# Opening the FFN's up products with the high terms, and moving proj_lo behind chunk 2's statistics

## The reference, cut to what matters

```python
x = L0_attn_x
x = x + 0.5 * ffn(_layernorm(x), W1, b1, W2, b2)        # FFN A
x = x + attn(_layernorm(x), w_qkv, w_out, b_out, proj)  # linear attention in blocks of 32
x = x + 0.5 * ffn(_layernorm(x), W1, b1, W2, b2)        # FFN B

def ffn(h, W1, b1, W2, b2):                             # W1 128x512, W2 512x128
    return relu(h @ W1 + b1) @ W2 + b2

def attn(x, w_qkv, w_out, b_out, proj):                 # 8 heads of 16, proj 8 x 16 x 128
    q, k, v = split(x @ w_qkv.T)                        # by head and block of 32 tokens
    qp, kp = elu(q @ proj) + 1, elu(k @ proj) + 1
    num = qp @ (kp.T @ v)
    return (num / (qp @ kp.sum() + 1e-8)) @ w_out.T + b_out
```

## Time and profile before

| what | us |
|---|---|
| median of 3 runs | 132.45 (132.33 to 132.54) |
| the profiled execution | 132.63 |
| its span on the core | 130.8 |
| PE busy | 120.4 (92% of the span) |
| DVE, ACT, POOL busy | 89.6, 90.0, 49.8 |

### The profile page before, as it was taken

The page is one execution under the profiler, slowest core; times in us unless marked ns, Lnnn a source line. Parts: engine busy times, 40 slices in busy tenths (PEclk is TensorE's granted clock), DMA queues, the critical chain, the costliest instruction groups (busy, mean ns, idle before and its releaser), DMA issues.

```text
span 130.8 us, 4453 instructions
## 1 busy us (share of the span) xinstructions
PE 120.4 (92%) x1895; PEld 97.1 (74%) x1895; DVE 89.6 (68%) x223; ACT 90.0 (69%) x154; POOL 49.8 (38%) x54
## 2 busy tenths in 40 slices
PE   5998999959999997999998999999969999999891
PEld 5887889825759964785985686699647788788891
DVE  6897884395699379769759948952793995437411
ACT  4764285778898686879778887888787774451720
POOL 7637659159139029005304930850000093005300
PEclk9999999999999999999999999999999999999999
DMA  4798400994009300001910000380020000200202
GB/s 108 227 274 223 75 3 0 351 202 93 0 8 351 135 0 0 5 5 41 382 63 0 8 5 0 147 331 9 5 80 5 5 3 5 77 3 0 85 1 80
DMA packets 10123, 11.10 MB, mean 85 GB/s; under 512 B 788, under 2 KB 6296, under 8 KB 10104
## 3 DMA queue, kind: packets, MB, share of 16 engines
q1 hardware_dynamic: 9952, 10.75, 26.5%
q10 hardware_dynamic: 152, 0.07, 0.2%
HBM read 2.03 MB, written 1.05 MB: 24 GB/s over the span
## 4 chain that ended last, share of the span: by engine, by line
PE 67%; DVE 14%; issue 8%; ACT 6%; POOL 3%; POOLq 0%; DVEq 0%
PE G L310 18%; PE wide L336 9%; PE SO L347 6%; ACT expo L643 5%; PE SO L363 5%; PE G L319 4%; PE G L292 3%; DVE feat L829 3%; PE SO L310 3%; PE G L301 3%; PE G L303 2%; PE G L302 2%; POOL rstd L986 2%; PE G L326 2%; DVE stats L795 2%
## 5 line engine op out<-in xcount | busy, mean ns | idle before, releaser
L829 DVE SCALAR_TENSOR_TENSOR feat<-expo,wide 128x1024 f32<-128x1024 f32 x32 | 38.7, 1218 | 18.7 <-ACT expo L643 18.3
L643 ACT ACTIVATE expo<-wide,minus_one 128x1024 f32<-128x1024 f32 x32 | 35.5, 1114 | 9.1 <-PE wide L336 9.0
L986 POOL TENSOR_TENSOR rstd<-var_eps,minus_half 128x4 f32<-128x4 f32 (+1 forms) x15 | 14.4, 962 | 64.8 <-DVE var_eps L802 64.5
L310 PE MATMUL G<-w,hidden 128*128 128x128 f32 x208 | 26.6, 277 | 0.0
L310 PEld LDWEIGHTS G<-w,hidden 128*128 128x128 f32 x208 | 25.1, 192 | 0.7
L336 PE MATMUL wide<-qk_packed,proj_padded 128*128 128x512 f32 x64 | 23.0, 444 | 0.5 <-DVE feat L829 0.3
L624 ACT ACTIVATE hidden<-G,b_cols 128x512 f32<-128x512 f32 (+1 forms) x25 | 15.9, 649 | 4.4 <-PE G L303 3.8
L347 PE MATMUL SO<-feat 128*32 128x32 f32 x1024 | 15.3, 197 | 1.4 <-DVE feat L829 1.3
L347 PEld LDWEIGHTS SO<-feat 128*32 128x32 f32 x1024 | 13.3, 111 | 2.3 <-DVE feat L829 1.7
L363 PEld LDWEIGHTS SO<-v_blocks,scores_sb 128*32 128x32 f32 x256 | 5.1, 107 | 11.3 <-issue 7.6
L301 PE MATMUL G<-xnT_hi,w_hi 128*128 128x512 f32 (+1 forms) x25 | 11.5, 459 | 1.2 <-DVE xnT_lo L816 1.2
(11 more groups left out here) (99 smaller groups left out, 192.8 us busy)
## 6 DMA issues: line engine op xcount, KB each, us to landing
qk_packed<-qk_hi SPq DMA_DIRECT2D x16, 256.0 KB, 2.5
qk_packed<-qk_lo SPq DMA_DIRECT2D x8, 256.0 KB, 2.5
qk_packed<-sixteenth SPq DMA_DIRECT2D x2, 512.0 KB, 6.3
x_in<-in_L_attn_x_dram SPq DMA_DIRECT2D x3, 256.0 KB, 5.1
out_dram<-x SPq DMA_DIRECT2D x3, 256.0 KB, 2.2
w<-in_L_ffn_W_dram SPq DMA_DIRECT2D x2, 256.0 KB, 3.9
x_in<-in_L_attn_x_dram SPq DMA_DIRECT2D x2, 128.0 KB, 2.5
proj_padded<-proj_hi SPq DMA_DIRECT2D x4, 64.0 KB, 2.4
```

The lines of the kernel that those rows point to most:

```text
L310: mm = pe.matmul(bank[:, t * D:(t + 1) * D], hidden[f][:, i, t * P:(t + 1) * P], w2[:, i, :], start=(i == 0 and t == tiles[0]), stop=(i == ...
L643: nc.scalar.activation(expo[:, n % 2, :, tokens(c)], wide[n % 2][:, :, tokens(c)], ACT.Exp, bias=minus_one[:, 0:1]).then_inc(exp_done, 1)
L829: nc.vector.scalar_tensor_tensor(out=feat[:, n % FEAT_BUFS, :, tokens(c)], in0=expo[:, n % 2, :, tokens(c)], scalar=1.0, in1=wide[n % 2][: ...
L986: nc.gpsimd.tensor_tensor(rstd[k][:, part], var_eps[k][:, part], minus_half[:, 0:n], ALU.pow).then_inc(rstd_ready[k], 1)
```

## The change

Three edits:

- `ffn_up` is divided into `up_hi_hi` (high x high, which waits for `xn_hi` alone) and `up_with_lo` (the other two products, with the wait for `xn_lo` between them, ahead of the third). `ffn_up` calls one after the other, so every up product of the kernel now waits for the low part at its third product.
- For the first half chunk of FFN A and for the first of the two last half chunks of FFN B, the four high x high products of the four quarters are issued ahead of the eight others. At the start `w1_lo_ready` is waited for after these four, and `w1_hi_ready` before them.
- The subtraction that makes `proj_lo` moves on DVE from ahead of `norm_apply(0, 2)` to behind `norm_stats(0, 3)`, the statistics of chunk 2.

```diff
-            def ffn_up(f, u, i, bank):
+            def up_hi_hi(f, u, i, bank):
...
                 if i == 0:
+                    wait(pe, xn_hi[k], u + 1)
+                pe.matmul(bank[:, part], w1_hi[:, cols], xnT_hi[k][:, part], start=True, stop=False)
+
+            def up_with_lo(f, u, i, bank):
...
+                pe.matmul(bank[:, part], w1_lo[:, cols], xnT_hi[k][:, part], start=False, stop=False)
+                if i == 0:
                     wait(pe, xn_lo[k], u + 1)
-                pe.matmul(bank[:, part], w1_hi[:, cols], xnT_hi[k][:, part], start=True, stop=False)
-                pe.matmul(bank[:, part], w1_lo[:, cols], xnT_hi[k][:, part], start=False, stop=False)
                 pe.matmul(bank[:, part], w1_hi[:, cols], xnT_lo[k][:, part], start=False, stop=True).then_inc(hidden_sum[f], 1)
+
+            def ffn_up(f, u, i, bank):
+
+                up_hi_hi(f, u, i, bank)
+                up_with_lo(f, u, i, bank)
...
-            pe.wait_ge(w1_lo_ready, 1)
+            pe.wait_ge(w1_hi_ready, 1)
             pe.wait_ge(b1_ready, 1)
             for i, bank in enumerate((W0A, W0B, GC, SO)):
-                ffn_up(0, 0, i, bank)
+                up_hi_hi(0, 0, i, bank)
+            pe.wait_ge(w1_lo_ready, 1)
+            for i, bank in enumerate((W0A, W0B, GC, SO)):
+                up_with_lo(0, 0, i, bank)
...
             for i, bank in enumerate((W1A, W1B, W0A, W0B)):
-                ffn_up(1, NC - 1, i, bank)
+                up_hi_hi(1, NC - 1, i, bank)
+            for i, bank in enumerate((W1A, W1B, W0A, W0B)):
+                up_with_lo(1, NC - 1, i, bank)
...
-            dve.wait_ge(proj_hi_ready, 1)
-            nc.vector.tensor_tensor(proj_lo[:, :, :], proj_small[:, :, :], proj_hi[:, :, :].bitcast(F32),
-                                    ALU.subtract).then_inc(proj_lo_ready, 1)
             norm_apply(0, 2, x_in[:, rows(1), :])
...
             dve.wait_ge(x_loaded[2], 16)
             norm_stats(0, 3, x_in[:, rows(2), :])
+            dve.wait_ge(proj_hi_ready, 1)
+            nc.vector.tensor_tensor(proj_lo[:, :, :], proj_small[:, :, :], proj_hi[:, :, :].bitcast(F32),
+                                    ALU.subtract).then_inc(proj_lo_ready, 1)
             for g, bank in enumerate((W1A, W1B)):
                 qk_lo_part(0, g, bank)
```

More of the change, by code:

```diff
@@ L299, in ffn_up @@
                 if i == 0:
+                    wait(pe, xn_hi[k], u + 1)
+                pe.matmul(bank[:, part], w1_hi[:, cols], xnT_hi[k][:, part], start=True, stop=False)
+            def up_with_lo(f, u, i, bank):
+                k, cols = 2 * f, slice(i * P, (i + 1) * P)
+                _, _, part = set_tiles(k, u)
+                pe.matmul(bank[:, part], w1_lo[:, cols], xnT_hi[k][:, part], start=False, stop=False)
+                if i == 0:
                     wait(pe, xn_lo[k], u + 1)
-                pe.matmul(bank[:, part], w1_hi[:, cols], xnT_hi[k][:, part], start=True, stop=False)
-                pe.matmul(bank[:, part], w1_lo[:, cols], xnT_hi[k][:, part], start=False, stop=False)
                 pe.matmul(bank[:, part], w1_hi[:, cols], xnT_lo[k][:, part], start=False, stop=True).then_inc(hidden_sum[f], 1)
+            def ffn_up(f, u, i, bank):
+                up_hi_hi(f, u, i, bank)
+                up_with_lo(f, u, i, bank)
             def ffn_down(f, u, i, bank):
```

## The result

| kernel | median of its runs, us | against the kernel before, 95% |
|---|---|---|
| before | 132.43 (132.33 to 132.54) | |
| with the change | 131.29 (131.20 to 131.46) | 0.9921 [0.9892, 0.9951] |
| the same two on a second chip | 131.42 against 132.40 | 0.9915 [0.9889, 0.9941] |

What follows compares the result with a forecast made beforehand. The chain was taken to run mostly over PE, with pauses in the opening, before the loop and at the end. 0.80 from the earlier loop start plus 0.46 at the end made 1.26: 132.45 to 131.2, range 130.9 to 132.0.

Steps and rivals of the forecast that it cites:

- Part 1: Opening: high products first make PE 0.43 earlier, but alone give nothing, as PE waits 0.4 longer for xn.
- Part 2: Opening: proj_lo and POOL's x_b and rstd delay each other; moving proj_lo starts xn 1.01 earlier, alone giving about 0.6.
- Part 1 and 2 together: Opening: high products first plus moving proj_lo start PE's next down products 1.0 earlier.
- Part 3: proj_lo's new place: fits DVE's idle time, but SP's queue cuts the DMA gain to 0.4; loop starts 0.8 earlier.
- Rival (a): Opening's gain lost in the DMAs of g = 0, possibly with POOL's rstd first: total -0.86 to -0.2; chance 0.18.
- Part 4: Inside the loop: the low-part wait at the third product is worth 0, both ways.
- Part 5: At the end: the first high product starts at 121.10 instead of 121.56, and 0.46 is kept.
- Rival (c): The end gives nothing because ACT's relus bound it: 131.65; chance 0.11 together with (d).
- (b): Slower, 132.9: proj_lo's 1.92 is its own length and the opening rstd's 2.02 has another cause; chance 0.07.
- (d): The loop gives the 0.8 back at a fixed event; chance 0.11 together with Rival (c).

Runs made afterwards that it cites:

- start_only: Kernel before with the low-part wait at the third product and the four high products first in the opening only: 131.61 against 132.34, 0.9955.
- proj_only: Kernel before with only proj_lo moved behind the statistics of chunk 2, products and waits unchanged: 132.04 against 132.34, 0.9991.
- after_again: The changed kernel with no further edit, profiled a second time: 131.42 against 132.40 for the kernel before, 0.9915.
- before_again: The kernel before with no edit, profiled a second time: 132.25 against 132.40, 0.9989.
- late_wait_only: Kernel before with only the low-part wait moved to every third up product, no products put first: 131.85 against 132.18, 0.9977.
- end_only: Kernel before with the low-part wait at every third product and the four high products first at the end only: 131.61 against 132.34, 0.9962.
- forced_sbuf: Kernel before with POOL's x_b made to wait for DVE's statistics of chunk 1, proj_lo keeping two SBUF inputs: 133.32 against 132.21, 1.0093.
- psum_input: Kernel before with proj_lo at its old place, written as zeros by a same-size instruction with one PSUM input: 132.17 against 132.34, 0.9987.

## Why the prediction was right, and where its steps were not

The time was forecast at 131.2 and is 131.29. The sum of 1.26 stands against 1.14. Point by point:

- **Part 1, "by itself this part gives nothing": wrong.** start_only gives 0.6 to 0.7, of which 0.16 is the later wait at the end. PE's own 0.43 was right (0.40 and 0.44 where the products of no use last alike). The step that failed is "PE then waits 0.4 longer for `xn` at 12.43": 12.43 belongs to the one course with the collision. In the others `xn` is there at 11.5 to 11.9, the two sums lie within a few tenths of each other, and an earlier PE is worth part of what it gains.
- **Part 2, the mutual wait: right as a mechanism, mis-sized as a share.** Forced, it costs 0.8 to 1.0, not less than the 0.6 forecast for this part alone. But taking it away alone brings 0.3 by the medians at most (proj_only), not told from nothing. It was expected to give 1.01 to `xn` in every run; two of eleven profiles have the course in which it can.
- **Part 1 and 2 together, 1.0 at the second down products:** in the same course the forecast held step by step. after_again has the first down products at 10.09 (forecast 10.06), `xn` at 11.47 (11.42) and the second down products at 12.81 (12.77). The profile of after came to 12.86 by another way, and by luck: the products of no use ended later, so the first high product came at 7.73 and not at 7.25, while b2 landed earlier and `xn` started at 11.04. Against before_again, which has the other course, the gain is only 0.4 (13.25 to 12.81).
- **Part 3: held.** `proj_lo` at 19.03 (forecast 19.0), 1.21 long (1.2), DVE ahead of POOL, `rstd` 1.92 long behind it at no cost, `qk_hi` at 21.43 (21.50), the first feature product at 25.34 with 0.60 of waiting for the DMA (25.4 and 0.7), the first `feature` at 27.23 (27.25). The 0.2 that it was to take from the 1.0 is about 0.15. Its "0.65 of the gain is spent in SP's queue" should be 0.6 by its own sum (1.0 less 0.4); nothing hangs on it. Rival (a), in which POOL comes first, is in none of the four profiles with the new place.
- **Part 4, "worth 0, both ways": right in the loop, incomplete outside it.** The loop is as long in all undisturbed profiles, 92.23 to 92.34. But the later wait does something at the end by itself, 0.16 (late_wait_only).
- **Part 5: held.** 0.46 forecast; 4.16 less 3.68 is 0.48, and less 3.77, as in after_again, 0.39. end_only gives 0.5 (1 less 0.9962, of 132.34), but with the later wait's share in the opening. Rival (c) is out.
- **Rivals (b) and (d)** are out by the 1.20 of `proj_lo` and by the equal length of the loop.

So the mechanism was right for the execution that it was read from, and the total was partly luck: the prediction took the gain of one course for that of the median. Worked out from before_again and after_again instead, without the clock's 0.9, it is 0.32 (27.51 to 27.19) and 0.38 (4.15 to 3.77), together 0.7; from the first pair of profiles it was 1.18. The measured 0.98 and 1.14 lie between, as they should for a mixture of both courses. How often each course comes up in the executions that were only timed is not known, and the length of the products of no use spreads the times as well.

On the port, the Trainium skill ("SBUF — State Buffer", section "Who interferes with whom") says that a DVE instruction with two SBUF inputs contends with a GpSimd instruction that reads SBUF, and calls the shared port pair an exclusive lock. The runs agree for `x_b` and `proj_lo` (2.34 when `x_b` is held; the two rows start 0.01 apart, `x_b` first, too close to say which had the port first) and for `proj_lo` ahead of `rstd` (1.92). They agree as well with the Trainium skill's rule, in the same section, that a DVE instruction with at most one SBUF input does not contend (1.28), and the Trainium skill's remark there that a `tensor_scalar` can contend as well fits the `var_eps` of 1.27 and the `xn` of 2.13. They differ in one case: with `rstd` ahead, at 10.20 to 11.24, `proj_lo` starts 0.23 later and still takes 1.20. There the measurement decides: this small `rstd` did not keep `proj_lo` waiting.

## What to carry to other kernels

A row that says two engines wait for each other tells of one execution. Before the wait is taken as the cause, look in a second profile of the same kernel for whether it is there, above all where the order of the two hangs on a DMA's arrival or on hundredths of a microsecond; if not, the edit is worth only the distance to the next limit behind it (here PE's own path). Where the later of two sums sets a time, write both down for each profile: it tells at once which edit can pay, and when the other takes over. And a wait for an operand in a group of accumulating products belongs at the product that uses it, with the others ahead, best of several banks at once: at this kernel's end that was 0.16 for the wait alone and 0.2 to 0.3 more for the order.

## What the runs showed of the hardware

- **POOL's `rstd` of 128 x 4 (1.04 us) lets a DVE subtraction with two SBUF inputs run beside it (1.20), but waits for it when that started first (1.92).** Of an addition of 128 x 512 on POOL and that subtraction, now one and now the other is held until the other's end (1.92 and 2.34).
- **A DVE instruction of 0.17 can be held for 1.27** by a POOL addition that began 0.05 before it, and so shift everything behind it.
- **The products of no use at PE's start do not take a fixed time**, though the profile gives a full granted clock there: 22 of them last from 4.23 (forced_sbuf) to 5.07. These two lines are from the timelines of before and of after:

```profile
1.55 4.32 PE L389 MATMUL wide<-ident 128*128 128x128 f32 x22 [1.55 <-POOL ident L1026]
```

```profile
1.55 5.07 PE L401 MATMUL wide<-ident 128*128 128x128 f32 x22 [1.55 <-POOL ident L1043]
```

Their spacing is 0.23 at first and 0.11 later, and the moment of the change differs from one execution to the next. With the old order the first down products start at 10.49 after 4.32 of them and at 11.09 after 5.06 (psum_input), 0.6 later, as much as the change's first part is worth. It may be the second cause of spread in proj_only; no execution of its slower group was profiled. The gain of start_only cannot be read from one pair of profiles for this reason, only from the medians.
- **The clock fell to its lower level at the loop's start**, in about one execution in eight with the old place of `proj_lo`, at a cost of 0.9 to 1.0 us in three profiles, after a stretch in which PE was busy about half of the time; after a like stretch it stayed in seven others.
